# Layer 3's cross attention: values kept 8 wide per head, division after the weighing, scores in two halves of two banks

## The reference, cut to what matters

```python
qh = rope(split(layernorm(x) @ w_q + b_q))      # 16 heads of 8
kh = rope(split(ctx @ w_k + b_k))               # 77 keys
vh = split(ctx @ w_v + b_v)
scores = einsum('bhqd,bhkd->bhqk', qh, kh) / sqrt(8)
scores = where(mask, scores, finfo.min)
attn = softmax(scores, axis=-1)
out = einsum('bhqk,bhkd->bhqd', attn, vh)       # 8 numbers per head
x = x + tanh(g) * (concat_heads(out) @ w_o + b_o)
```

## Time and profile before

| | us |
|---|---|
| median of 3 runs | 1049.45 (1048.04 to 1050.45) |
| span of the profiled execution | 1057.6 |
| its stretch from the end of layer 2's last expert matmul to the last update of layer 3's attention | 911 to 1020 |
| steps 3 to 15 of the attention's loop (start of score to start of score) | 943.49 to 1003.16 |
| feed-forward part of layer 3, to the end | 1020 to 1057.6 |

### The profile page before, as it was taken

How to read it: one execution, slowest core, us unless ns; L and a number is a source line. 1 busy time by engine, 2 the same in 40 slices (tenths; PEclk the granted TensorE clock), 3 DMA queues, 4 the chain that set the end, 5 groups by cost and what they waited for, 6 DMA issues and landing times.

```text
span 1057.6 us, 19542 instructions
## 1 busy us (share of the span) xinstructions
PE 919.4 (87%) x6337; PEld 655.6 (62%) x6337; DVE 785.7 (74%) x2080; ACT 557.7 (53%) x1494; POOL 490.0 (46%) x451
## 2 busy tenths in 40 slices
PE   6898985888778999869997598988989999989987
PEld 4787533767578989727775243434437677768774
DVE  6889999999756777769998376777734744589982
ACT  4675456886444445724443156766764233445533
POOL 5444553555066564635556777574530600024430
PEclk9999896999879999969999659989999999999998
DMA  9300000000111111410000322222102000000001
GB/s 324 149 1 1 2 6 1 1 1 1 41 39 39 41 40 33 109 66 1 0 1 0 107 67 62 82 76 62 31 1 101 1 1 1 1 2 2 1 1 40
DMA packets 29828, 40.55 MB, mean 38 GB/s; under 512 B 11468, under 2 KB 25036, under 8 KB 29228
## 3 DMA queue, kind: packets, MB, share of 16 engines
q1 hardware_dynamic: 27244, 34.28, 10.3%
q0 software_dynamic: 2496, 5.16, 1.9%
HBM read 31.44 MB, written 7.82 MB: 37 GB/s over the span
## 4 chain that ended last, share of the span: by engine, by line
PE 27%; issue 14%; POOL 7%; DVE 5%; ACT 3%; SPq 1%; DMA 0%; DVEq 0%; POOLq 0%; ACTq 0%
POOL att L1787 6%; PE ps L1163 4%; PE ps L829 4%; PE ps L1135 4%; PE ps L819 4%; PE ps L1147 3%; PE ps L793 1%; PE ps L1249 1%; PE ps L1257 1%; DVE rs L2124 1%; PE ps L1101 1%; DVE stats L2001 0%; SPq L570 0%; PE ps L1106 0%; DVE U L2029 0%
## 5 line engine op out<-in xcount | busy, mean ns | idle before, releaser
L1787 POOL TENSOR_TENSOR att<-att,ri 128x1232 f32<-128x1232 f32 x64 | 169.3, 2645 | 190.5 <-DVE ri L2130 190.5
L793 PE MATMUL ps<-VW,PT 128*128 128x128 f32 (+3 forms) x1280 | 157.6, 278 | 17.5 <-DVE x L2145 16.0
L793 PEld LDWEIGHTS ps<-VW,PT 128*128 128x128 f32 (+1 forms) x1280 | 148.4, 192 | 35.2 <-DVE x L2145 28.3
L1369 ACT ACTIVATE PT<-ps 128x512 f32<-128x512 f32 x128 | 70.6, 594 | 89.5 <-PE ps L766 88.7
L766 PE MATMUL ps<-W,att 128*128 128x128 f32 (+1 forms) x640 | 86.9, 282 | 16.2 <-POOL att L1787 14.7
L1761 POOL TENSOR_TENSOR rstd<-ve,minus_half 128x4 f32<-128x4 f32 x38 | 38.8, 1039 | 114.2 <-DVE ve L2016 97.7
L900 PE MATMUL ps<-PT,att 128*128 128x128 f32 x624 | 80.8, 285 | 8.5 <-issue 8.4
L829 PEld LDWEIGHTS ps<-U,att 128*128 128x128 f32 x512 | 66.3, 191 | 33.1 <-issue 29.1
L766 PEld LDWEIGHTS ps<-W,att 128*128 128x128 f32 (+1 forms) x640 | 72.7, 143 | 22.3 <-POOL att L1787 15.5
L2581 DVE CUSTOM_DVE_ANT_0 C<-ps,cmaskb 128x512 bf16<-128x512 f32 (+1 forms) x128 | 71.1, 555 | 20.7 <-PE ps L1135 18.0
L2581 DVE CUSTOM_DVE_ANT_0 U<-ps,cmaskb 128x384 bf16<-128x384 f32 (+1 forms) x128 | 53.9, 421 | 41.8 <-PE ps L1135 41.5
(11 more groups left out here) (432 smaller groups left out, 2105.6 us busy)
## 6 DMA issues: line engine op xcount, KB each, us to landing
U<-in_ffn SPq DMA_DIRECT2D x1, 6176.0 KB, 23.2
U<-split SPq DMA_DIRECT2D x144, 32.0 KB
W<-split SPq DMA_DIRECT2D x144, 32.0 KB
W<-in_packed SPq DMA_DIRECT2D x1, 2162.5 KB, 23.5
U<-in_ffn SPq DMA_DIRECT2D x1, 2060.0 KB, 9.7
U<-in_moe SPq DMA_DIRECT2D x1, 2048.0 KB, 7.3
split<-VBD SPq DMA_DIRECT2D x4, 384.0 KB, 2.9
split<-W SPq DMA_DIRECT2D x4, 384.0 KB, 2.7
```

What stands on the lines that cost most here:

```text
L793: q = mm(attended(s, t), PT[0:m, t.slot(2), c, :], batch(VW, t.group)[0:m, c * D:(c + 1) * D], start=(c == 0), stop=(c == NC - 1))
L1369: go(PT[:, t.slot(2), 4 * k:4 * k + 4, :].rearrange("p c n -> p (c n)"), ps[:, k0 + k, :], ACT.Copy).then_inc(probsT, 1)
L1787: tt(p, p, over_keys(ri[:, t.slot(2), :]), ALU.mult).then_inc(probs, 1)
```

## The change

Layer 3's attention is a new function `narrow` on each engine; layers 0 to 2 keep `cross`.

- Values stay 8 wide per head: `VBG` holds, per group of four heads, keys by 32 numbers; `value_blocks` transposes it (three transposes per batch, two ScalarE copies) in place of `fold_values`' ten chunks. `w_o` is applied at the end (`project`), and `b_o` is added to x by GpSimd (`add_bias`).
- `weigh`: per tile, for the values (a = 0) and for a table of ones (a = 1, which gives the sums), three key chunks of 128, 128 and 52 rows, each as four matmuls of 32 output rows, one per group: 24 matmuls of 128 columns. Tiles are taken in pairs of a `tail_bank` (6 or 7).
- After a pair: ScalarE copies the bank (`take_sums`), TensorE turns the sums (`turn_sums`), VectorE inverts 32 numbers per token, GpSimd spreads them to 256 (`spread_inverse`), TensorE transposes that (`turn_inverse`), VectorE multiplies (`scale`), TensorE applies `w_o` (`project`), VectorE adds to x (`update`).
- Scores are made in two halves of two groups (two banks). Each half has a semaphore count of its own in `scores`, `rowmax` and `shifted`. The mask is added with 32 rows per group instead of with the full identity. Queries are read from `FT`, without the copies to `qs`.
- The exponentials are turned in 12 transposes per tile instead of ten (four groups of 128, 128 and 52 columns), over two banks instead of three; `total` and `normalize` are gone.
- 96 more columns are loaded at the start; other semaphores are merged.

```diff
@@ TensorE
-                t.then_inc(vw_ps, 1)      # fold_values(X3): removed for all four batches
+            def value_blocks(s, b):
+                for c in range(2):
+                    pe.transpose(ps[:, bank, c * P:(c + 1) * P], VBG[:, b, c * P:(c + 1) * P], ident)
+                pe.transpose(ps[0:REST, bank, 2 * P:3 * P], VBG[:, b, 2 * P:GK], ident).then_inc(vw_ps, 1)
+                def score(t):
...
+                    for half in range(2):
+                        wait(pe, shifted, n0 + 2 * t + half)
+                        for g in (2 * half, 2 * half + 1):
+                            mm(ps[:, g, 0:GK], FT[rows, t * P:(t + 1) * P], KBG[rows, b, :], start=True, stop=False)
+                        for g in (2 * half, 2 * half + 1):
+                            m = mm(ps[:, g, 0:GK], share[rows, :], nb3[rows, b, g * GK:(g + 1) * GK], start=False, stop=True)
+                        m.then_inc(scores, 1)
+                def weigh(t):
...
+                    for a in range(2):
+                        for c in range(3):
+                            pe.wait_ge(probsT, 3 * (n0 + t) + (5 if c < 2 else 6))
+                            for g in range(RG):
+                                m = P if c < 2 else REST
+                                lhs = VN[0:m, t // TB, c, rows_of_group(g)] if a == 0 else w("ones")[0:m, 32 * c:32 * c + 32]
+                                z = mm(ps[rows_of_group(g), tail_bank(q), (2 * a + i) * P:(2 * a + i + 1) * P], lhs, ...)
+                for k in range(NT + 4):
+                    if k < NT:
+                        score(k)
+                    if k == 0:
+                        rotate(B - 1)
+                    if 0 <= k - 2 < NT:
+                        weigh(k - 2)
+                    if 0 <= k - 1 < NT:
+                        turn_piece(k - 1, 0)
+                        turn_piece(k - 1, 1)
+                    if k >= 5 and k % 2 == 1:
+                        project((k - 5) // 2)
+                    if k >= 4 and k % 2 == 0:
+                        turn_inverse((k - 4) // 2)
+                    if k >= 3 and k % 2 == 1 and (k - 3) // 2 < NT // 2:
+                        turn_sums((k - 3) // 2)
+                    if 0 <= k - 1 < NT:
+                        turn_piece(k - 1, 2)
@@ VectorE
+                for k in range(NT + 5):
+                    if k >= 6 and k % 2 == 0:
+                        update((k - 6) // 2)
+                    if k >= 5 and k % 2 == 1:
+                        scale((k - 5) // 2)
+                    if k >= 4 and k % 2 == 0 and (k - 4) // 2 < NT // 2:
+                        invert((k - 4) // 2)
+                    if k < NT:
+                        for half in range(2):
+                            largest(k, half)
+                            shift(k, half)
+                    if k == 0:
+                        rope3(B - 1)
```

More of the change, by code:

```diff
@@ L87 @@
 AHEAD = 2
+REST = GK - 2 * P
+SLOTS_OF_SCORES = 3
 UNIT0 = 2
@@ L745, in score @@
                             m = mm(ps[:, g, 0:GK], qs[rows, t.slot(2), :], batch(KBG, t.group)[rows, :],
[L746 to L750, removed]
+                                   start=True, stop=True)
                     m.then_inc(scores, 1)
@@ L1219, in _ @@
             q3(0)
-            pe.wait_ge(kv_chain, 5)
-            fold_values(X3, w("3wo"), 0)
+            for b in range(3):
+                value_blocks(X3, b)
             starts(pe, X3)
@@ L1391, in cross @@
                     return stage, lambda: skewed_loop(act, steps, NT, TB)
-                def stage_last(t):
-                    if isinstance(t.n, int) and t.n == TB - 1:
-                        act.wait_ge(roped, B)
-                    if not isinstance(t.n, int) or t.n >= 2:
-                        stage(t)
-                if s == X3:
-                    steps = [(stage_last, -1), (evacuate, 3), (exponent, 1), (late_fold, 0)]
-                    return stage, lambda: skewed_loop(act, steps, NT, TB)
@@ L1715, in _ @@
             queries3(0)
-            fold_values(X3, 0)
+            for b in range(3):
+                value_blocks(X3, b)
             queries3(1)
             turned_x3(2)
-            fold_values(X3, 1)
+            value_blocks(X3, 3)
             queries3(2)
-            act.wait_ge(roped, 1)
-            stage3(Tile(None, TB, 0))
             turned_x3(3)
             queries3(3)
-            stage3(Tile(None, TB, 1))
-            last_cross()
+            narrow(X3, HD ** -0.5)
             starts(act, F3)
@@ L1985, in _, with spread_inverse, add_bias @@
             t.then_inc(kbd, 1)
-            roots(X3)
-            cross(X3)
+            def spread_inverse(s):
+                for q in range(NT // 2):
+                    pool.wait_ge(recip, tiles_before(s) + 2 * q + 2)
+                    pool.tensor_copy(inverse[:, q % 2, :].rearrange("p (i h d) -> p i h d", i=2, d=HD),
+                                     ri2[:, q % 2, :, :].unsqueeze(3).to_broadcast([P, 2, H, HD])).then_inc(staged, 2)
+            def add_bias(s, b):
+                pool.wait_ge(s_xn, TB * (ROUND0[s] + b + 1))
+                pool.wait_ge(x_biased, 1)
+                xb = x[:, b * TB:(b + 1) * TB, :]
+                tt(xb, xb, w(f"{LAYER[s]}bo").unsqueeze(1).to_broadcast([P, TB, D]), ALU.add).then_inc(x_biased, 1)
+            for b in range(B):
+                root(ROUND0[X3] + b, b)
+                if b >= 1:
+                    add_bias(X3, b - 1)
+            add_bias(X3, B - 1)
+            spread_inverse(X3)
             roots(F3)
@@ L2645, in _ @@
             rope3(2)
-            cross(X3)
+            narrow(X3)
             starts(dve, F3)
@@ L2708, in _pad, with _same_head @@
     return out
+def _same_head(first, row, n=P):
+    out = np.zeros((P, 32), np.float32)
+    for r in range(n):
+        h = (first + r) // KEYS
+        out[row + r, h * HD:(h + 1) * HD] = 1.0
+    return out
 def _pack(i):
```

193 lines of the change are left out of this document (155 added, 38 removed).

## The result

| | before | after |
|---|---|---|
| median of 4 runs | 1049.95 (1048.04 to 1050.97) | 1041.52 (1039.76 to 1044.55) |
| time of the profiled execution | not among the data | 1043.15 |
| its span | 1057.6 | 1041.4 |
| first turn of the stage's queries to the end of the last update | 912.79 to 1020.02: 107.2 | 900.92 to 1003.49: 102.6 |

The ratio is 0.992, 95% interval 0.9902 to 0.9939: 8.4 us faster. The span of before's profile is 7.6 us over its median time. That is not the change: before any work that the change touches but a load at the start, at VectorE's same instruction in the MoE stage, it stood at 819.55 and the changed kernel at 810.36, 9.2 apart; a kernel whose code is that of before up to there reached it at 811.44, and all twelve other profiles of this document lie between 809.0 and 812.9. So spans can't be subtracted here; only stretches can.

A forecast was written before the change was run, and what follows sets the result against it. TensorE and VectorE were both taken as near their limit in the loop, TensorE also ahead of it. Savings by step 4 (5.3), in later steps and at the end summed to -7.5 from 1049.45: 1042.0 us, range 1036 to 1050.5.

The forecast's parts named there:

- Entry: Ahead of layer 3's attention loop: without the value folds on TensorE, the first maximum comes 3.5 us earlier, at 925.7.
- TensorE sets the step: Steady attention loop: TensorE's work, not VectorE's, decides the time per tile, 4.9 us against 4.97 before.
- Score: TensorE's score matmuls and mask per tile, both halves running together, with the change into their layout: 0.96 us.
- the rival of serial halves: Score matmuls: the second half waits for the first, 5.5 us per step, kernel 1049.2; chance 0.20.
- Weighting: TensorE's `weigh` per tile: twelve rounds of matmuls plus layout changes, 1.70 us where the product took 2.2.
- the rival of 4.4: Steady loop: no layout change for 52 rows and no waits, 4.4 us per step, kernel 1036; chance 0.12.
- the slower rival: `weigh`: a round of four matmuls takes 0.22 us, step 6.2, kernel 1058.6; chance 0.15.
- Turns: TensorE's twelve transposes of the exponentials per tile, 1.32 us, plus 0.09 for a layout change: 1.41.
- Pair work with the bank's wait: TensorE per tile: `turn_sums`, `turn_inverse` and `project`, 0.55 us, plus 0.13 mean wait for the first copy of transposes.
- VectorE: Steady loop: VectorE's work falls to 3.9 us per step, halves 0.80 each, leaving 1 us to spare.
- The end: Start of step 16 to the last update, through the last pair's chain over the engines: 10.4 us.
- Half clock: TensorE's clock halving while the loop fills: one such stretch more costs 1.7 us, one less gains as much.

The follow-up runs named there:

- second profile: The changed kernel itself, unchanged, run and profiled once more in a later group: 1041.23 us, ratio 0.9914 to the kernel before.
- second group: Later set of runs in which the unchanged changed kernel was timed again beside the kernel before: 1041.23 against 1050.97 us.
- the profile with small matmuls: Fifty small matmuls that nobody reads added in the first two steps of layer 3's attention, against the changed kernel: 1041.73 us, ratio 0.9901 to before.

## Why the prediction was right, and where it was not

The time was forecast at 1042.0 and came to 1041.52; the sum behind it was -7.5, all in the attention stage. By stretch:

| stretch | forecast | first profile | second profile |
|---|---|---|---|
| first turn to start of step 4 | -5.3 | -3.0 | -5.6 |
| step 4 to step 15 | -0.6 | -1.5 | -1.5 |
| step 15 to the last update | -1.6 | -0.2 | -0.3 |
| stage | -7.5 | -4.7 | -7.3 |
| MoE stage | 0 | -2.7 | -2.7 |

(Stage before: 35.86, 54.51, 16.86. First profile after: 32.83, 53.03, 16.71. Second: 30.28, 53.03, 16.59. In the first profile 32.83 carries the 10.2 us at half clock. The MoE row of the second profile: 816.41 to 903.41, 87.00.)

- **Entry: right.** First maximum 3.5 earlier forecast, 3.9 found. The folds were on the path in full, as their return showed (4.8 in the profile, 4.1 in the times).
- **TensorE sets the step: right.** 4.9 forecast, 4.83 found; even and odd steps 4.7 and 5.1 forecast, 4.68 and 4.99 found. Leaving TensorE's work out shortened the step; joining VectorE's halves, which leaves it fewer instructions, did not. The four terms below (0.87, 1.85, 1.46, 0.65) add up to the 4.83 by themselves: the 0.15 that the forecast kept for waits had nothing to answer to, and the terms were 0.08 too small together.
- **Score, 0.96 forecast: 0.87.** The halves overlapped, so the rival of serial halves (5.5 per step) is out. The Trainium skill, page TensorE: Matmul & The Clock Gate, section on what overlaps in packed matmuls, has matmuls in strict program order; in the trace the second half's records start at 957.79 and the first half's masks, which stand ahead of them in the program, at 958.39, so the trace does not agree, and here the measurement decides.
- **Weighting, 1.70 forecast: 1.85.** A term that was mis-sized: three changes of layout at 0.09 were taken, 0.11 to 0.15 were found. The bound 0 for 52 rows (the rival of 4.4) fell, and turned out to be the gain that lay there for whoever keeps the rows at 128. Rounds of four matmuls took 0.11 (0.21 for two), as in the earlier trace rows, so the slower rival (0.22 per round) is out.
- **Turns, 1.41 forecast: 1.46. Pair work with the bank's wait, 0.68 forecast: 0.65.** (0.81 in odd steps, 0.48 in even ones, of which 0.26 is the wait for the first copy, as forecast: 966.41 to 966.89 for two records of 0.11.)
- **VectorE: right, a little too high.** Halves 0.80 each; busy 3.66 per step, 3.9 forecast; waits 1.07 and 0.85 us per step for the first half.
- **The end, 10.4 from step 16 forecast: 11.7.** The chain over five engines at the end was counted too short: TensorE waits 1.05 for GpSimd and 0.59 for VectorE, VectorE then 1.38 for TensorE. Some 0.6 of the 1.3 is half clock, which began at 1000.3 here and which before did not have in this place: in the profile with small matmuls, at full clock to the last update, the same end took 11.1. What is left, 0.7, is the chain itself. Fourteen tiles hide it, the last pair doesn't.
- **Missed: the MoE stage, 2.7.** The narrower blocks were read as work of an engine with room, so they were costed at nothing. What counted was not GpSimd's time but what ran beside it.
- **The 96 columns more: nothing that shows.** 0.3 us at most was allowed; the load landed in 3.9 us instead of 4.0, and TensorE's first load of weights came at 5.87 (6.08 in the second profile) instead of 6.00.
- **Half clock: the size taken (one stretch more or less, 1.7) was right for some executions** (3.4 us in the first steps before and in the changed kernel's second profile), and too small for others: 10.2 in the first profile, which cost what the missed term gave. That execution alone would have put the gain of the stage at 4.7.

The mechanism was right, and that the time came out 0.5 us from the forecast is partly luck. The 7.5 stood for the attention stage alone, where the second profile has 7.3; inside it the loop gave 0.9 more than forecast and the end 1.3 less. The MoE stage's 2.7 was not in the sum. In the second group the changed kernel was 9.7 us faster than before, which is near 7.3 and 2.7 together, so the forecast was 2 us short there. In the first group it was 8.4 faster: two of its four runs, 1043.15 and 1044.55, had mean clocks of 0.925 and 0.924, the lowest of its ten, and the forecast was counted from 1049.45, 0.5 under the median of before in that table.

## What to carry to other kernels

When an array is used in several layouts, count the changes of layout as work of their own and pad small chunks with zeros where that removes some: here that was worth 0.40 us per step, where the change itself gave 0.16 in the steady loop. When GpSimd gets less to do, look at what VectorE does in those same microseconds before you put the gain at nothing. Take two profiles before a stretch of a few us is explained by the kernel.

## What the runs showed of the hardware

- A VectorE operation with two inputs in SBUF, beside a GpSimd multiplication of 1232 columns, took until about the end of that one: started at 824.86 and done at 827.27, where GpSimd's ran to 826.93; 1.90 instead of 0.48 for the next such one. With one input in PSUM it took 0.48 either way. The Trainium skill, page SBUF — State Buffer, section Who interferes with whom, says that the two engines lock a shared pair of ports for a whole instruction when VectorE has two SBUF inputs and GpSimd reads SBUF; the traces here agree, with 2.41 against 0.87 us. By that rule the prediction could have asked what VectorE does beside the narrower blocks.
- Matmuls with 52 rows instead of 128 are not shorter, and 0.11 to 0.15 us go at each change. The Trainium skill, page TensorEngine Tiling (Array Packing), section Key Properties, says that a change of tiling mode drains the engine; the trace agrees, if 52 rows are another mode than 128, and puts the number on it.
- The granted clock differs between executions of one kernel. Of the changed kernel's ten timed runs the four over 1042 had mean clocks of 0.924 to 0.929 over the program, the five under 1041 had 0.931 to 0.937. In the table of stages above, 6.8 us more at half clock went with 2.7 to 3 us more in the stage, and with 128 rows the same 3.4 us went with 1.5 us more when they lay over step 2 instead of step 1.
